# Four attention layers in one program: layer 1's first projections placed beside layer 0's last scores, with two gates instead of two barriers

## The reference, cut to what matters

```python
x = _L0_xattn_ref(x, mask, ctx, mask, Wq, bq, Wk, bk, Wv, bv)          # [8, 256, 512]
#   per head (16 of 16 channels): attn = softmax(q k / 4, key mask); mean = attn v; ex2 = attn v*v
#   std = sqrt(relu(ex2 - mean*mean)); out = (masked instance norm of x * std + mean) * mask
x = _L1_xattn_ref(ctx, x, mask, ...)    # 256 latents (layer 0's output) on 256 context rows and themselves:
#   h = concat([ctx, latents]); q = latents @ q_w; k, v = h @ kv_w; 16 heads of 32; softmax
#   attn_out @ out_w + out_b + latents; rmsnorm; MLP with gelu; + latents
x = _L2_xattn_ref(x, ctx, mask, ...)    # 32 query heads on 8 key heads, layer norm
x = _L3_xattn_ref(x, ctx, ...)          # positions, layer norms, 16 heads, gelu MLP
```

## Time and profile before

| | us |
|---|---|
| median of 3 runs (lowest, highest) | 3317.26 (3314.80, 3321.52) |
| the profiled execution | 3316.17 |
| its span | 3314.4 |
| TensorE busy | 2816.2 (85%) |
| VectorE busy | 1860.3 (56%) |
| ScalarE busy | 1329.2 (40%) |
| POOL busy | 872.1 (26%) |

### The profile page before, as it was taken

How to read it: one execution, slowest core, us unless ns; L and a number is a source line. 1 busy time by engine, 2 the same in 40 slices (tenths; PEclk the granted TensorE clock), 3 DMA queues, 4 the chain that set the end, 5 groups by cost and what they waited for, 6 DMA issues and landing times. The chain is left out here.

```text
span 3314.4 us, 41358 instructions
## 1 busy us (share of the span) xinstructions
PE 2816.2 (85%) x14624; PEld 1319.0 (40%) x14624; DVE 1860.3 (56%) x4546; ACT 1329.2 (40%) x2326; POOL 872.1 (26%) x690
## 2 busy tenths in 40 slices
PE   4888888867999999998999999986568888888895
PEld 1222222214555555556656555542222333233332
DVE  3777777733334444301455655566867776667641
ACT  0555555552333333222333233422215544454562
POOL 1566666661344444420000010101111010100000
PEclk7999999988999999799999999987779899999897
DMA  4444444321002101213223232323333232323210
GB/s 98 96 96 96 99 99 98 81 64 60 21 27 71 38 27 34 71 39 83 53 60 61 63 69 55 67 61 84 75 82 86 69 77 57 89 55 74 65 34 20
DMA packets 182335, 219.92 MB, mean 66 GB/s; under 512 B 40841, under 2 KB 135665, under 8 KB 175985
## 3 DMA queue, kind: packets, MB, share of 16 engines
q1 hardware_dynamic: 170064, 189.74, 24.9%
q0 software_dynamic: 6016, 20.98, 1.9%
q10 hardware_dynamic: 6048, 6.56, 0.6%
HBM read 146.90 MB, written 51.64 MB: 60 GB/s over the span
## 5 line engine op out<-in xcount | busy, mean ns | idle before, releaser
L1259 DVE TENSOR_REDUCE l_M<-PS 128x1 f32<-128x512 f32 x512 | 329.4, 680 | 170.1 <-PE PS L722 169.7
L1485 DVE TENSOR_REDUCE l_M<-PS 128x1 f32<-128x512 f32 x512 | 334.7, 683 | 142.2 <-PE PS L967 138.8
L1198 ACT ACTIVATE l_P<-PS 128x512 f32<-128x512 f32 x512 | 286.7, 598 | 255.7 <-PE PS L977 237.7
L1558 POOL TENSOR_TENSOR l_S<-l_P 128x512 f32<-128x512 f32 x256 | 325.6, 1305 | 58.4 <-ACT l_P L1050 58.4
L1050 ACT ACTIVATE l_P<-PS 128x512 f32<-128x512 f32 x512 | 276.0, 598 | 136.6 <-PE PS L731 134.5
L967 PE MATMUL PS<-l_KS,l_QS 97*128 97x512 bf16 x512 | 205.2, 411 | 103.8 <-DVE l_M L1485 72.4
L1324 DVE TENSOR_REDUCE l1a_M<-PS 128x1 f32<-128x512 f32 x256 | 158.8, 681 | 206.3 <-PE PS L784 206.3
L722 PE MATMUL PS<-l_KS,l_QS 97*128 97x512 bf16 x512 | 202.0, 404 | 81.7 <-DVE l_M L1259 41.9
L1163 ACT ACTIVATE l_P<-l_P 128x1024 f32<-128x1024 f32 x128 | 135.2, 1057 | 299.5 <-DVE l_P L1405 299.1
L1391 DVE CUSTOM_DVE_ANT_0 l_JK<-PS,l_MK 128x256 f32<-128x256 f32 x512 | 195.8, 419 | 101.0 <-PE PS L897 98.8
L612 PE MATMUL PS<-l_YT,l_w_mlp_w 128*128 128x256 f32 x1024 | 235.9, 387 | 5.0 <-ACT l_YT L1125 4.9
(11 more groups left out here) (244 smaller groups left out, 4769.7 us busy)
## 6 DMA issues: line engine op xcount, KB each, us to landing
l_QS<-q_scratch SPq DMA_DIRECT2D x128, 128.0 KB, 5.6
q_scratch<-l_T SPq DMA_DIRECT2D x96, 128.0 KB
l_QS<-q_scratch SPq DMA_DIRECT2D x32, 384.0 KB, 4.9
k_scratch<-l_T SPq DMA_DIRECT2D x96, 128.0 KB
l_KS<-k_scratch SPq DMA_DIRECT2D x32, 384.0 KB
l_QS<-q_scratch SPq DMA_DIRECT2D x32, 256.0 KB, 5.6
l_KS<-k_scratch SPq DMA_DIRECT2D x32, 256.0 KB
l_RB<-l_recs SPq DMA_DIRECT2D x32, 256.0 KB
```

The lines of the kernel that those rows point to most:

```text
L1198: e.activation(t.P[quad % 4][:, m, :], PS[:, COUNTS.bank[st], :], ACT.Exp, scale=0.25).then_inc(q.sem("act.exp", st), 1)
L1259: e.tensor_reduce(t.M[i % 2][:, qt, hd:hd + 1], PS[:, COUNTS.bank[st], :], AX.X, ALU.max).then_inc(q.sem("dve.smax", st), 1)
L1485: e.tensor_reduce(t.M[i % 2][:, qt, hd:hd + 1], PS[:, COUNTS.bank[st], :], AX.X, ALU.max).then_inc(q.sem("dve.smax", st), 1)
L1558: x = e.tensor_tensor(t.S[j % 2][:, m, :], t.P[2 * j % 4][:, m, :], t.P[(2 * j + 1) % 4][:, m, :], ALU.add)
```

## The change

The two barriers go. All layers' steps are placed on one axis, with layer 1 beginning at 18.35; the changed code no longer has `merge` and `pipeline`, and layer 0's steps stand at the positions they had (the last steps unsqueezed, at 19.8 to 20.5).

- Gate 3 at 17.6 holds ScalarE, POOL and SP until all work up to 17.4 is done; behind it come `1.start` (weights for keys, queries and values, one row of biases, one memset) at 17.61 and the load of batch 0's latents and context at 17.65.
- Transposes, key, query and value projections of layer 1's item 0 stand at 18.35 to 19.16.
- Gate 4 at 19.6 holds ScalarE, VectorE, POOL and SP until all work up to 19.4 is done; behind it comes `1.start2` (output weights, the other row, POOL's memsets, one memset). The mask has a step of its own (`1.mload`).
- Maxima of item 0 stand at 19.81 to 20.11 instead of 1.05 to 1.65 behind the layer's begin, and wait for layer 0's last exponential and its last copy of sums. Item 1's projections are at 19.45 to 20.16, item 0's first score step at 20.5.
- The mask row is made with one VectorE instruction instead of two.
- Tiles of layer 0 and a few of layer 1 get other addresses, so that what layer 1 writes early lies over tiles that layer 0 has done with.

```diff
-    return pipeline((a0, a1, a2, c, p), ((0.0, 1.0),) * 5, keep=True)
+    order = [(2 * b + h + beat + at, st) for b, h in ITEMS for beat, part in enumerate((a0, a1, a2, c, p)) for at, st in part(b, h)]
+    return order + [(-9, ("0.start", 0, 0, 0)), (17.4, ("mark", 3, 0, 0)), (19.4, ("mark", 4, 0, 0))]
+BEGIN1 = 18.35
+def layer1_order():
         if h == 0:
-            at = -0.9 if b else 0.0
-            out += [(at, k("load")), (at + 0.15, k("mrow"))] + [((0.6 + at) if b else 0.05, k("lat", 0)), ((0.7 + at) if b else 0.08, k("lat", 1))]
+            out += [(-0.9 if b > 1 else -0.7, k("load")), (-0.6 if b else 1.2, k("mload")), (-0.5 if b else 1.27, k("mrow"))]
+            out += [(-0.3 if b else 0.0, k("lat", 0)), (-0.2 if b else 0.03, k("lat", 1))]
-        out += [(1.05 + 0.2 * n, k("smax", n)) for n in range(4)] + [(1.8, k("rows")), (1.81, k("turn"))]
+        out += [((1.05 + 0.2 * n) if (b, h) > (0, 0) else (1.46 + 0.1 * n), k("smax", n)) for n in range(4)] + [(1.8, k("rows")), (1.81, k("turn"))]
-    order = [x for x in order if first(x)] + [(1, ("barrier", 0, 0, 0))] + [x for x in order if not first(x)]
+    return order + [(-0.75, ("gate", 3, 0, 0)), (-0.74, ("1.start", 0, 0, 0)), (1.25, ("gate", 4, 0, 0)), (1.25, ("1.start2", 0, 0, 0)),
+                    (18.95, ("mark", 2, 0, 0))]
...
+    places = ((0, layer0_order()), (BEGIN1, layer1_order()), (BEGIN1 + BEGIN2, layer2_order()),
+              (BEGIN1 + BEGIN2 + 18.3, layer3_order()))
+    order = sorted([(begin + at, st) for begin, steps in places for at, st in steps], key=lambda x: x[0])
...
-GATED = {0: ("pe", "sp", "pool"), 1: ("pe", "sp"), 2: ("pe", "act", "dve", "pool", "sp")}
+GATED = {3: ("act", "pool", "sp"), 4: ("act", "dve", "pool", "sp"), 0: ("pe", "sp", "pool"), 1: ("pe", "sp"), 2: ("pe", "act", "dve", "pool", "sp")}
...
             elif kind == "1.smax":
-                q.wait_ge("pool.start", ("1.start", 0, 0, 0))
+                q.wait_ge("pool.start", ("1.start2", 0, 0, 0))
...
+                q.wait_ge("act.exp", ("0.sc", B - 1, 1, 31))
+                q.wait_ge("act.sums", ("0.sout", B - 1, 1, 1))
...
-                q.next_needs(e.tensor_scalar(t.MF[:, :], t.MI[:, :], 0.0, None, ALU.not_equal))
...
-                e.tensor_scalar(t.MB[b % 2][:, 0:256], t.MF[:, :], -1.0, NEG, ALU.add, ALU.mult).then_inc(q.sem("dve.mask", st), 1)
+                e.tensor_scalar(t.MB[b % 2][:, 0:256], t.MI[:, :], 0.0, -NEG, ALU.is_equal, ALU.mult).then_inc(q.sem("dve.mask", st), 1)
...
             elif kind == "1.load":
                 q.wait_ge("pstore", step("1.f2", i - 5))
+                q.wait_ge("store", ("0.f5", b, 1, 1))
...
             elif kind == "2.start2":
                 q.wait_ge("mrow", ("1.mrow", B - 1, 0, 0))
-                q.wait_ge("pe.sc", ("1.sc", B - 1, 1, 3))
+                q.wait_ge("pe.vals", ("1.vals", B - 1, 1, 7))
```

More of the change, by code:

```diff
@@ L14 @@
 NEG = 1e30
[L19 to L56, removed]
 def layer0_order():
@@ L114, in steps @@
         return out
-    order = sorted([(2 * b + h + at, st) for b, h in ITEMS for at, st in steps(b, h)] + merge((tail[0], 0.0, 0.8)), key=lambda x: x[0])
-    first = lambda x: x[0] < 1 or x[1][0][0] == "0"
-    order = [x for x in order if first(x)] + [(1, ("barrier", 0, 0, 0))] + [x for x in order if not first(x)]
-    return order + [(18.95, ("mark", 2, 0, 0))]
+    order = [(2 * b + h + at, st) for b, h in ITEMS for at, st in steps(b, h)]
+    return order + [(-0.75, ("gate", 3, 0, 0)), (-0.74, ("1.start", 0, 0, 0)), (1.25, ("gate", 4, 0, 0)), (1.25, ("1.start2", 0, 0, 0)),
+                    (18.95, ("mark", 2, 0, 0))]
 BEGIN2 = 16.75
@@ L475, in build_program @@
             l0.MT = sb("MT", [24, 512], bf16)
-            l0.P = [sb(f"P{i}", [128, 4, 512]) for i in range(4)]
+            l0.P = [P0] + [sb(f"P{i}", [128, 4, 512]) for i in (1, 2, 3)]
             l0.S = [sb(f"S{i}", [128, 4, 512]) for i in range(2)]
[L478 to L490, removed]
+            l0.X = [pair("X0"), X1, pair("X2")]
+            l0.ME, l0.EX = [pair("ME0"), ME1], [pair("EX0"), EX1]
             l0.sums = [dram(f"l0_sums{i}", [8, 512]) for i in range(4)]
@@ L814, in tensor1 @@
                 if kt == 0:
-                    q.wait_ge("act.vals", step("1.out", i, 0) if g else step("1.out", i - 1, 1))
+                    q.wait_ge("act.vals", step("1.out", i, 0) if g else step("1.out", i - 1, 1) if i else ("0.out", B - 1, 1, 1))
                 q.wait_ge("act.exp", step("1.sc", i, j // 2))
@@ L1129, in scalar2 @@
                 q.wait_ge("dve.v", ("1.v", B - 1, 1, 3))
-                q.wait_ge("dve.mask", ("1.load", B - 1, 0, 0))
+                q.wait_ge("dve.mask", ("1.mload", B - 1, 0, 0))
                 q.wait_ge("pstore", ("1.f2", B - 3, 1, 0))
@@ L1338, in vector1 @@
             elif kind == "1.f1":
+                q.wait_ge("rows", ("1.start2", 0, 0, 0))
                 q.wait_ge("pe.f1", st)
@@ L1581, in gpsimd1 @@
                 e.dma_start(t.H[b % 2][:, :, 0:256], tokens(I["ctxT"][b])).then_inc(q.sem("inc", st), 16)
-                q.wait_ge("dve.mask", step("1.load", i - 2))
+            elif kind == "1.mload":
+                q.wait_ge("dve.mask", step("1.mload", i - 2))
                 e.dma_start(t.MI[:, :], I["mask1"][b:b + 1, :]).then_inc(q.sem("inm", st), 16)
@@ L1731, in sync1 @@
                 row(q, t.vb, "vb1")
+            elif kind == "1.start2":
                 row(q, t.ob, "ob1")
             elif kind == "1.mrow":
-                q.wait_ge("pool.start", ("1.start", 0, 0, 0))
+                q.wait_ge("pool.start", ("1.start2", 0, 0, 0))
                 q.wait_ge("pe.sc", step("1.sc", i - 3, 3))
-                q.wait_ge("dve.mask", step("1.load", i))
+                q.wait_ge("dve.mask", step("1.mload", i))
                 for m in range(4):
```

81 lines of the change are left out of this document (47 added, 34 removed), and 4 rows, old and new, of tables (LATER, MOVES).

## The result

| | before | after |
|---|---|---|
| median of 5 runs (lowest, highest), us | 3318.18 (3314.80, 3331.31) | 3304.13 (3296.90, 3308.14) |
| ratio of the runs, 95% interval | | 0.9953 (0.9934 to 0.9972) |
| the profiled execution, us | 3316.17 | 3304.13 |

A forecast was written before the change was run, and what follows sets the result against it. TensorE was taken to bound the kernel, idling in two holes around layer 0's end. First scores 45.8 us earlier, less 1.5 and 3, gave 41.3 off 3316.2: 3274.9 us profiled, 3276 as a median, range 3264 to 3295.

The forecast's parts named there:

- part 2: First gate, at 17.6, and the weight loads behind it: last item's scores delayed 1.5 us (bounds 0 and 8).
- What bounds the kernel: TensorE, full from 822.3 us, with two holes before, together 33.4 us; earlier first scores of layer 1 shorten the end equally.
- Part 1: Layer 1's projections beside layer 0's last scores: stretch ends at 741 instead of 733.9, costing 7 us there.
- Part 3: Second gate to layer 1's first maxima: gate opens at 748, maxima start at 756 instead of 789.50, 33.5 us earlier.
- Part 4: Layer 1's first maxima to first scores: 20.5 us, so first scores at 776.5 instead of 822.27, 45.8 earlier.
- Part 5: Layer 0's tail beside layer 1's fill, ahead of its first exponentials: costs 3 us (bounds 0 and 9).
- (a): Second gate: copies, memsets and mask rows land late, maxima start at 764; 3284 us. Chance 0.24 for this, (b) or both.
- (b): Layer 0's end: weight loads and tail come on the path, 12.5 us, 3288. Chance 0.24 for this, (a) or both.
- (c): Around the layer 0 to 1 turn: projections fill every wait and the clock stays at 2.4 GHz; 3266 us. Chance 0.11.
- (d): All of layer 0: the new layout lengthens POOL's folds, 3354 us if all showed. Chance 0.04.
- (e): At the gates: they hold as the barriers did, for a transfer placed too early; about 3317 us. Chance 0.03.

The follow-up runs named there:

- e5: e1 with layer 1's output weights and batch 1's load issued by POOL only once the mask rows have landed; 3285.26 us, ratio 0.9912.
- e10: e5 with batch 1's one-row mask load issued by POOL ahead of the held-back loads; 3272.72 us, ratio 0.9868.
- e1: Changed kernel with layer 1's maxima split put ahead of the next item's last value add on VectorE; 3286.53 us, ratio 0.9906.
- b1: e1 run again unchanged, in the rounds of e10; 3277.37 us, ratio 0.9877 to the kernel before.
- e2: Changed kernel with layer 0 moved down instead of the others up, so ties in layers 1 to 3 fall as before; 3283.38 us, ratio 0.9894.
- e7: e2 with layer 1 and its gates begun at 19.3 instead of 18.35; 3303.23 us, ratio 0.9965.
- e4: Changed kernel with each POOL fold of layer 1 split into four instructions of 256 columns; 3311.90 us, ratio 0.9977.

## Why the prediction was wrong, step by step

The miss is 29.2 us in the profiled executions (3304.1 against 3274.9). It is made of 12.7 at the first scores (790.67 against 778.0, which is 776.5 and the 1.5 of part 2), -1.6 in the tail, 14.6 behind it, and 3.5 behind 1350, where two executions of one kernel differ by more.

- **What bounds the kernel**: right for where it was read, and wrong for what it was used for. "Since the engine is saturated behind them, every microsecond [...] is one off the end" holds only while the order of the engines' lists behind that point stays. This is the step that failed most, by 14.6 us, and without it the time would have been inside the range. I took the sum of positions for an exact one; the steps on either side of the tie are nowhere in the diff. The prediction's own sign for it, a layer 1 that is not full after the fill, came true: 69.17 us busy of 77.70.
- **Part 1** (ends at 741): too low by some 4. Layer 1's keys begin at 746.40; 1.5 of that is part 2. The rest are five waits of 0.62 to 1.40 us for ScalarE's exponentials between 697 and 745, and a low clock at the start, 0.50 from 697 to 703 and 0.68 from there to 707. The term is within my bounds of 3 to 17 us. POOL, busy 25.34 us of these 43 instead of 35.05, was no limit.
- **Part 2** (1.5): right in its number, in part by luck. The last item's scores begin at 697.32, 1.52 later. What small transfers pay beside the weights I had too small: a 16 KB fetch takes 6.1 us to land (the same step took 1.5 before), and 32 KB copies 5.2 where the earlier trace rows have 1.9. I had read that 1.9 as measured while large loads ran, but those copies were issued up to 734, and the loads from 736 on. Most of the extra time goes into the slack ahead of the row maxima. DMA issues, 675 to 695:

```profile
l1a_w_v_w<-in_v_w ACTq DMA_DIRECT2D x1, 1024.0 KB, 14.1
...
l_ME<-l_E SPq DMA_DIRECT2D x4, 32.0 KB, 5.2
...
l_l0r<-l_sums SPq DMA_DIRECT2D x1, 16.0 KB, 6.1
```

  From what the Trainium skill says of queues that are served a packet at a time in turn (DMA: Bandwidth & Descriptors, "Queues, rings and completion order") I had put this term under 1 us. The trace agrees with the rule in that a small transfer passes a large one: the fetch, issued at 683.71, 6.7 us behind the third weight, landed 1.3 us ahead of it. But it did not pass for nothing, at 6.1 us where it took 1.5.
- **Part 3** (gate 748, mask rows 755 to 757, maxima 756): late by 8.4. Some 4.5 are the last value step (744.55, put at 740) and 1.5 the slower gate; with it POOL's memsets come at 754.14. The rest is the landing of the mask rows: 5.3 us with 2 MB beside them. The row that I had for this (3.7) was of a time with less in flight. The maxima came at 764.38, just outside my bound of 764. e5 and e10 show that the loads are the cause of the slow landing: 1.8 and 1.9 us without them. That VectorE's list could stand for the next batch's mask had no term at all; it is what took e5's gain.
- **Part 4** (20.5): 26.3, near the upper bound of 27. More than half of the 5.8 us over follows from part 3: after the 4.47 us wait the clock is at 0.50 from 764 to 777, and the first two maxima steps stand 5.1 and 5.8 us from the next where I had 3.2. In e10, which has no such wait, first maxima to first scores is 23.1, still 2.6 over. A pitch of 3.2 is too short, and I had no reason to go below the 3.9 of the earlier trace rows: with the reductions of a step 2.48, a value add and the reciprocal between them, the reductions stand 3.9, 4.9 and 3.9 apart (758.32, 762.23, 767.09, 771.00).
- **Part 5** (3): 1.4 (31.6 earlier at the first scores, 30.2 at 825). The square root's table load runs on ScalarE, from 787.51, beside a key projection on TensorE.
- **Rivals.** (a) is what happened at the fill: maxima at 764. Its 3284 stands among the 3277 to 3287 that the kernel takes with the tie mended (e1, b1, e2), but not for its reason alone: 4.5 of the 8.4 us came from the later last value step (parts 1 and 2), and the 5.8 of part 4 are not in it. (b) did not come: part 2 as forecast, a small tail. (c) no: waits of 4.47, 5.61 and 5.28 us were left, each with a low clock behind it. (d) is refuted: the difference at 650 is -0.2, and the folds, take 1312 ns where they took 1305:

```profile
L1533 POOL TENSOR_TENSOR l_S<-l_P 128x512 f32<-128x512 f32 x256 | 327.9, 1312 | 68.0 <-ACT l_P L1022 68.0
```

  (e) no; e7, with its gate behind the tail, shows a part of it. No rival of mine had a step that gets slower in a part of the program that the change leaves alone.

The mechanism of the forecast, work of layer 1 in the two holes, was right, and it is worth nearly its size once both faults are mended: in its trace e10 wins 38.9 us up to 825 and keeps them up to 1350, against 41.3 forecast, and its ratio of 0.9868 is 3273.5 on the 3317.26 of before.

## What to carry to other kernels

Where an order comes from sorting computed positions, equal keys are decisions: after a shift of all positions compare each engine's list with the old one step by step, far from the edit too, and break ties by numbers that cannot round away. When a barrier becomes a gate, look at what the gate releases at once: a 1 KB transfer that the next stage waits for must be issued, and have landed, ahead of the megabytes that nobody needs yet, and the same is true of every other small transfer on the same queue.

## What the runs showed of the hardware that I had not expected

- An instruction of VectorE on 16 columns, 0.19 us alone, lasts until the end of a POOL instruction that started 0.12 us earlier: 2.28 us beside a fold of 2.34, 0.66 beside pieces of 0.69. Started 0.45 us behind a fold's start, it takes 1.95.
- A transfer of 1 KB lands in 1.8 us with nothing large in flight, in 5.3 beside 2 MB on other queues, and in 6.6 behind 2 MB on its own (e5); 1 MB takes 5.6.
- TensorE falls to 1.2 GHz after waits of 4.5 to 5.6 us; after a wait of 0.69 (e10) it stays at 2.4 GHz for most of the fill (mean clock 0.93 from 757 to 780, against 0.50 from 764 to 777 in the changed kernel). Shorter waits can do it too: in e4, of six waits of 2.14 or 2.15 us three have a low clock behind them, and in the changed kernel of six waits of 1.32 at the same places none has.
